# Edge attention in a four-layer graph kernel: masked maxima two steps further ahead, shifts in two operations, head sums normalised and added straight from PSUM

## The reference, cut to what matters

```python
s_u = x @ W_u.T + b_u
s_v = x @ W_v.T
e = s_u[src] + s_v[dst]
e = jnp.where(e >= 0, e, 0.2 * e)
m = jax.ops.segment_max(e, dst, num_segments=n_nodes)
e_exp = jnp.exp(e - m[dst])
denom = jax.ops.segment_sum(e_exp, dst, num_segments=n_nodes)
probs = e_exp / denom[dst]
xh = x.reshape(n_nodes, head_dim, num_heads)
msg = xh[src] * probs[:, None, :]
out = jax.ops.segment_sum(msg, dst, num_segments=n_nodes)
```

## Time and profile before

| What | Value |
|---|---|
| median of 3 runs | 995.82 us (993.37 to 998.53) |
| the profiled execution | 998.12 us, span 996.3 us |
| mean granted TensorE clock | 0.953 |
| PE / DVE / ACT / POOL busy over the span | 906.0 / 437.5 / 281.7 / 183.9 us |
| first copy of u (ACT) to the next layer's first operation on DVE | 525.4 to 608.9 us |

### The profile page before, as it was taken

The page is one execution under the profiler, slowest core; times in us unless marked ns, Lnnn a source line. Parts: engine busy times, 40 slices in busy tenths (PEclk is TensorE's granted clock), DMA queues, the critical chain, the costliest instruction groups (busy, mean ns, idle before and its releaser), DMA issues.

```text
span 996.3 us, 15288 instructions
## 1 busy us (share of the span) xinstructions
PE 906.0 (91%) x5607; PEld 730.9 (73%) x5607; DVE 437.5 (44%) x1375; ACT 281.7 (28%) x629; POOL 183.9 (18%) x179
## 2 busy tenths in 40 slices
PE   7999998999999999899997778999999998899895
PEld 7997656889999767788876667777886554565863
DVE  6687655522222421542278976423335242240422
ACT  5110362122222113233338952332112111114210
POOL 2100000122221100045317850000101100000231
PEclk9999999999999999999988988999999998799998
DMA  9202001288884603159341000354000000330694
GB/s 327 98 1 64 1 1 43 88 297 313 326 327 163 226 0 127 52 180 310 102 160 69 1 2 1 126 190 146 13 1 16 17 1 1 126 120 8 213 397 162
DMA packets 27452, 119.96 MB, mean 120 GB/s; under 512 B 5414, under 2 KB 9420, under 8 KB 19583
## 3 DMA queue, kind: packets, MB, share of 16 engines
q1 hardware_dynamic: 22012, 103.90, 29.3%
q0 software_dynamic: 5376, 15.20, 4.5%
HBM read 106.11 MB, written 12.98 MB: 120 GB/s over the span
## 4 chain that ended last, share of the span: by engine, by line
PE 75%; DVE 13%; DMA 4%; issue 4%; ACT 3%; POOL 1%; SPq 1%; DVEq 0%; POOLq 0%; ACTq 0%
PE PS L779 8%; PE PS L450 6%; PE PS L427 6%; PE PS L596 5%; PE PS L794 4%; PE PS L844 4%; PE PS L830 4%; PE PS L461 4%; PE PS L521 3%; PE PS L912 2%; PE PS L1213 2%; PE PS L866 2%; PE PS L901 2%; DVE ring L1904 2%; DVE w L1923 2%
## 5 line engine op out<-in xcount | busy, mean ns | idle before, releaser
L427 PE MATMUL PS<-const 128*128 128x128 f32 x726 | 98.9, 298 | 5.8 <-DVE X L1290 2.1
L427 PEld LDWEIGHTS PS<-const 128*128 128x128 f32 x726 | 94.4, 211 | 10.4 <-DVE X L1290 2.8
L779 PE MATMUL PS<-HT,ring 128*128 128x128 f32 x680 | 79.1, 275 | 3.3 <-DVE HT L1444 1.7
L779 PEld LDWEIGHTS PS<-HT,ring 128*128 128x128 f32 x680 | 78.4, 192 | 4.6 <-issue 3.9
L2548 POOL TENSOR_TENSOR col<-col,power 125x4 f32<-125x4 f32 (+2 forms) x13 | 11.9, 917 | 335.8 <-DVE col L1283 246.3
L2608 POOL DMA_INDIRECT slot_rows<-ST,route x43 | 43.4, 1009 | 154.7 <-ACT ST L2319 96.0
L2645 POOL TENSOR_TENSOR arena<-arena,ring 125x625 f32<-125x625 f32 x40 | 56.2, 1426 | 25.4 <-ACT arena L2406 13.0
L1829 DVE TENSOR_TENSOR HT<-HT,PS 128x256 f32<-128x256 f32 (+1 forms) x51 | 19.1, 377 | 89.8 <-ACT HT L2308 71.6
L596 PE MATMUL PS<-HT 125*125 125x250 bf16 x470 | 51.3, 270 | 1.0 <-DVE HT L1699 1.0
L596 PEld LDWEIGHTS PS<-HT 125*125 125x125 bf16 x470 | 50.2, 136 | 1.1 <-DVE HT L1699 1.1
L794 PE MATMUL PS<-ring,HT 128*128 128x256 f32 x204 | 46.8, 380 | 0.0
(11 more groups left out here) (460 smaller groups left out, 1691.4 us busy)
## 6 DMA issues: line engine op xcount, KB each, us to landing
ring<-in_experts SPq DMA_DIRECT2D x17, 1386.0 KB, 6.2
ring<-in_experts SPq DMA_DIRECT2D x17, 768.0 KB, 6.2
ring<-in_experts SPq DMA_DIRECT2D x11, 1026.0 KB, 7.7
arena<-in_experts SPq DMA_DIRECT2D x10, 1024.0 KB, 9.6
ring<-in_experts SPq DMA_DIRECT2D x7, 1024.0 KB, 8.2
arena<-in_experts SPq DMA_DIRECT2D x6, 1026.0 KB, 8.1
arena<-in_gnn SPq DMA_DIRECT2D x5, 1024.0 KB, 5.8
ring<-in_experts SPq DMA_DIRECT2D x8, 513.0 KB, 3.5
```

The costliest lines, as they stand in the source:

```text
L427: pe.matmul(PS[:, bank, 0:128], ident, ident, start=True, stop=True)
L779: mm = pe.matmul(PS[:, bank, at:at + SLOTS], both[:, j, k, m * 128:(m + 1) * 128], xs[0][i % 2][:, k, :], start=(k == 0), stop=(k == KD - 1))
```

## The change

Four things are changed, all in this stage.

1. The maxima of head h >= 3 start at DVE's step 5h-9, two steps earlier than before, and those of head 2 end one step earlier. Two waits are added for it, since buffers are reused sooner: a maximum waits for the POOL sum ten steps before it, and a head's shifts wait for the last exponential of the head two before it.
2. The shifts take two operations, and only the biased one is stored.
3. `take_y` and heads_y are gone. DVE reads the transposed sums in PSUM: for eight (head, tile) pairs one maximum and one reciprocal, then eight operations of 125 x 32 that multiply and add to X. This happens at DVE's steps 13, 21, 29 and 37, and for the last eight pairs behind the last count.
4. The last bank's transposes go to banks 1 and 0, where both went to bank 1.

```diff
@@ masked, shifts @@
                     dve.wait_ge(u_full, h + 2 if h else 1)
+                    if h >= 2:
+                        dve.wait_ge(bent_ready, i - 2 * NT + 1)
...
-                    link(dve.scalar_tensor_tensor(low[j][:, t0:t1], umax[j][:, t0:t1], -0.2, v08[:, t0:t1, h],
-                                                  ALU.mult, ALU.add))
-                    link(dve.scalar_tensor_tensor(shift[j][:, 0, t0:t1], umax[j][:, t0:t1], -1.0, low[j][:, t0:t1],
-                                                  ALU.mult, ALU.min))
-                    dve.tensor_tensor(shift[j][:, 1, t0:t1], shift[j][:, 0, t0:t1], v08[:, t0:t1, h],
-                                      ALU.subtract).then_inc(shift_ready, 1)
+                    if h >= 2:
+                        dve.wait_ge(gat_exp, NT * (h - 1))
+                    link(dve.scalar_tensor_tensor(low[j][:, t0:t1], umax[j][:, t0:t1], -1.0, v08[:, t0:t1, h],
+                                                  ALU.mult, ALU.subtract))
+                    dve.scalar_tensor_tensor(shift[j][:, t0:t1], umax[j][:, t0:t1], -0.2, low[j][:, t0:t1],
+                                             ALU.mult, ALU.min).then_inc(shift_ready, 1)
@@ normalise becomes add_sums @@
-                    link(dve.tensor_tensor(o, y[:, :, 0:32], rden.unsqueeze(2).broadcast_to([TP, b - a, 32]), ALU.mult))
-                    for h in range(h0, h1):
-                        xs = X[:, :, :].rearrange("p t (c h) -> p h t c", h=NX)[:, h]
-                        ins = dve.tensor_tensor(xs, xs, heads_y[:, h * NT:(h + 1) * NT, 0:32], ALU.add)
+                    xs = X[:, :, :].rearrange("p t (c h) -> p h t c", h=NX)
+                    for j in range(j0, j1):
+                        h, t = divmod(8 * b + j, NT)
+                        ins = dve.scalar_tensor_tensor(xs[:, h, t], y[:, j, 0:32], gate_flat[:, 120 + j:121 + j], xs[:, h, t],
+                                                       ALU.mult, ALU.add)
@@ DVE's order @@
-                ahead_of = {0: (5, 6), 1: (7, 8), 2: (9,)}
-                for h in range(2, NX):
+                ahead_of = {0: (5, 6), 1: (7, 8), 2: (9,), 3: (10, 11), 4: (12, 13), 5: (14,)}
+                for h in range(3, NX):
                     for j, ts in enumerate(((0, 1), (2,), (3,), (4,))):
-                        ahead_of[NT * h - 7 + j] = tuple(NT * h + t for t in ts)
+                        ahead_of[NT * h - 9 + j] = tuple(NT * h + t for t in ts)
...
-                    if i in (24, 32):
-                        dve.wait_ge(gat_y, i // 8 - 1)
-                        link(normalise_taken(i // 4 - 6, i // 4 - 4))
+                    if i >= 13 and i % 8 == 5:
+                        dve.wait_ge(gat_turned, i // 8)
+                        add_sums(i // 8 - 1, 0, 8).then_inc(gat_y, 1)
@@ ACT @@
-                    if i >= 12 and i % 8 == 4:
-                        take_y(i // 8 - 1, 8)
```

More of the change, by code:

```diff
@@ L274, in build @@
         XH = view(HT, 0, TP, NT, NX * 64)
-        heads_y = view(HT, NT * NX * 64, TP, NX * NT, 33)
         uvT = HT[0:40, 3900:3900 + N]
@@ L284, in build @@
         maskb = view(MB, 0, TP, NT, N)
-        shift = [view(col, 200 + 16 * j, TP, 2, NT) for j in range(2)]
+        shift = [col[:, 200 + 16 * j:200 + 16 * j + NT] for j in range(2)]
         gate_flat = gate[:, :, :, :].rearrange("p a t e -> p (a t e)")
@@ L1011, in turn_output @@
                     for k in pairs:
-                        mm = pe.transpose(PS[0:TP, b % 2 if b < 4 else 1, k * 128:(k + 1) * 128], sums_t[:, b % 2, k * TP:(k + 1) * TP],
+                        mm = pe.transpose(PS[0:TP, b % 2 if b < 4 else 1 - part, k * 128:(k + 1) * 128], sums_t[:, b % 2, k * TP:(k + 1) * TP],
                                           ident)
@@ L1924, in count_edges, with add_sums @@
                                       ALU.mult).then_inc(gat_pt, 1)
[L1926 to L1931, removed]
-                    link(dve.reciprocal(rden, den))
-                    link(dve.tensor_tensor(o, y[:, :, 0:32], rden.unsqueeze(2).broadcast_to([TP, b - a, 32]), ALU.mult))
-                    for h in range(h0, h1):
-                        xs = X[:, :, :].rearrange("p t (c h) -> p h t c", h=NX)[:, h]
-                        ins = dve.tensor_tensor(xs, xs, heads_y[:, h * NT:(h + 1) * NT, 0:32], ALU.add)
-                    return ins
-                def normalise_taken(h0, h1):
-                    return normalise(h0, h1, heads_y[:, h0 * NT:h1 * NT, :])
+                def add_sums(b, j0, j1):
+                    y = PS[0:TP, b % 2 if b < 4 else int(j0 == 0), :].rearrange("p (t c) -> p t c", c=64)
+                    den, rden = gate_flat[:, 80 + j0:80 + j1], gate_flat[:, 120 + j0:120 + j1]
+                    link(dve.tensor_scalar(den, y[:, j0:j1, 32], 1e-30, None, ALU.max))
+                    link(dve.reciprocal(rden, den))
+                    xs = X[:, :, :].rearrange("p t (c h) -> p h t c", h=NX)
[3 more added lines that the diff above has]
+                                                       ALU.mult, ALU.add)
+                    return ins
                 link(masked(0))
@@ L1965, in layer2_gnn @@
                             shifts(m // NT, 0, NT)
-                    if i in (24, 32):
-                        dve.wait_ge(gat_y, i // 8 - 1)
-                        link(normalise_taken(i // 4 - 6, i // 4 - 4))
+                    if i >= 13 and i % 8 == 5:
+                        dve.wait_ge(gat_turned, i // 8)
+                        add_sums(i // 8 - 1, 0, 8).then_inc(gat_y, 1)
                 count_edges(steps - 1)
[L1970 to L1973, removed]
+                dve.wait_ge(gat_turned, 5)
+                add_sums(4, 0, 6)
                 dve.wait_ge(gat_turned, 6)
-                ins = normalise(NX - 1, NX, PS[0:TP, 1, 192:512].rearrange("p (t c) -> p t c", t=NT))
+                ins = add_sums(4, 6, 8)
                 ins.then_inc(gat_taken, 1)
@@ L2413, in exponential @@
                         act.wait_ge(gat_tr, i - 2)
-                    act.activation(ex[:, i % 3, :], bent[:, i % 3, :], ACT.Exp, bias=shift[h % 2][:, 1, t:t + 1],
+                    act.activation(ex[:, i % 3, :], bent[:, i % 3, :], ACT.Exp, bias=shift[h % 2][:, t:t + 1],
                                    scale=0.2).then_inc(gat_exp, 1)
@@ L2423, in take_sums @@
                     act.activation(sums_t[:, b % 2, c0:c0 + c], PS[:, b % 2, c0:c0 + c], ACT.Copy).then_inc(gat_sums, 1)
[L2425 to L2430, removed]
                 for i in range(3):
@@ L2443, in layer2_gnn @@
                         take_sums(i // 8 - 1, 0, 4)
-                    if i >= 12 and i % 8 == 4:
-                        take_y(i // 8 - 1, 8)
                 take_sums(4, 0, 3)
-                take_y(4, 3)
                 take_sums(4, 3, 1)
```

## The result

| | before | changed |
|---|---|---|
| median of 8 runs | 994.99 us (992.78 to 999.12) | 1001.90 us (999.92 to 1006.58) |
| ratio | | 1.0063, 95% interval 1.0039 to 1.0088 |
| profiled execution, span | 998.12, 996.3 us | 999.92, 998.0 us |

The changed kernel is slower by 0.6%, 1001.9 us against 1001.8 predicted. That agreement is luck in part: the stage itself grew twice as much as forecast, and the rest of the program was shorter. In the table of the experiments, the medians and ratios leave out two executions that were in a slow state, one of e2 (4988.26 us) and one of e6 (1001.48 us).

A forecast was written before the change was run, and what follows sets the result against it. ACT and DVE were both full, PE set the pace at the end, and the new order made a ring bind. Terms -0.4 + 6.3 - 2.0 + 2.1 = +6.0 us on 995.82 gave 1001.8 us, range 990 to 1008.

The forecast's parts named there:

- The mechanism: At heads 3 to 7 DVE's earlier maxima wait for ACT's copy of u, 1 to 3 us each.
- the walk: Waits added through ACT, DVE and PE from one copy of u to the next: 10.4, 12.65, 9.56 and 12.6 us.
- The sum in the prediction: Copies of u for heads 3 to 7 span 45.2 us against 38.97 before, taken as +6.3.
- The term of 2.1 us: Two stretches of PE at 1.2 GHz, with one output each on the path, add 2.1 us.
- The tail: From the copy of u for head 7 to the next layer: 28.3 us against 30.28, so -2.0.
- The sums' price: On DVE, eight pairs with their maximum and reciprocal take 1.8 us; lower end 1.4, upper 3.45.
- the rival in which POOL slows them: DVE's small operations are slow beside POOL: eight pairs take 3.45 us instead of 1.8, total 1007.4 us; chance 0.13.
- my upper end: Upper bound for eight pairs on DVE: 3.45 us, what the first normalisation took beside POOL.
- The two rivals that would have made it faster or equal: Faster: the ring does not bind, 988.6 us, chance 0.14. Equal: gain and loss cancel, 996.1 us, chance 0.18.
- the ring: Loop from copy of u through DVE's counts, PE's turns and ACT's exponentials to the next copy: 9.5 us against 7.7.

The follow-up runs named there:

- e2: The changed kernel with the order of the maxima of before, parts 2 to 4 alone; stage 75.6 and 78.2 us, ratios to before 0.9883 and 0.9911.
- e6: The changed kernel with the sums' copy, transposes and additions to X two steps later on all three engines; stage 86.7 us, ratio to before 0.9968.
- e1: The kernel before with only the maxima two steps further ahead and the two waits that go with it; stage 100.3 us, ratio to before 1.0119.
- e3: The changed kernel with the copy of u for heads 3 to 7 two exponentials earlier on ACT; stage 85.1 us, ratio to before 0.9954.
- e5: The changed kernel with 16 idle products on PE at each of six waits, 96 in all; stage 91.7 us, ratio to before 1.0046.
- e8: e2 with each of the 40 small multiply-adds done twice, the extra result not used; stage 84.8 us, ratio to before 1.0035.

## Why the prediction was right, and where it was not

**The mechanism was right.** DVE waits for the copy of u at each of heads 4 to 7, 9.0 us in four waits (1 to 3 us each were forecast); at head 3 it waits 0.88 us, which the trace puts down to a POOL sum that ended as the copy did. Take_sums waited 2.52 us (2.3 walked). e1 and e2 show that the order is the loss, 17 us by itself and 17 to 20 us on top of e2, and e3 that the copy's place on ACT makes 10 us of it. For the other 7 to 9.5 us the walk has no wait of its own.

**The walk's waits.** For the heads 3 to 7 it had 10.4, 12.65, 9.56 and 12.6; the trace 10.8, 13.8, 11.0 and 14.8. The fillers, with the full clock, gave 9.56 and 12.50 for the last two, as walked. For the first two they don't bear it out: head 3 to 4 took 11.0 before the fillers began, at a clock of 0.85, and head 4 to 5 took 14.75, since the fillers themselves stood on its path. So two of the four lengths are confirmed. The sum in the prediction has a slip in it: 45.2 less 38.97 is 6.2, not 6.3.

**The clock was mis-sized.** The term of 2.1 us, two stretches with an output each, was too small by 2 to 6 us: the walk at the full clock gives 83.5 + 3.9 = 87.4 us for the stage, the trace 95.3, the difference is 7.9, and e5 gave 3.8 back net of its own products. The 4.1 us between the two are not assigned by any run. Not only outputs are slow in such a stretch: two turns took 2.46 us instead of 1.35, and I had counted none. There were also more stretches than two: over the whole stage the granted clock was 0.82 and 0.84 in the changed kernel, and 0.90, 0.90 and 0.88 in the kernel before.

**The tail** was 31.1 us against 28.3 walked, again with clock below full. The last addition did shorten the end: from the last count to the next layer are 3.8 us (612.23 to 616.05) against 4.8, 1.0 where I had 1.1.

**The sums' price was right**: 1.86 us against 1.8, and 0.18 us from one small operation to the next. At the first eight (550.45 to 552.31) POOL stood still from 550.60 to 552.15, so they don't settle the rival in which POOL slows them. The second eight do. Here they are, with POOL's row beside them:

```profile
572.34 0.16 DVE L1931 TENSOR_SCALAR gate<-PS 125x8 f32<-125x8 f32 x1
572.77 1.52 DVE L1936 SCALAR_TENSOR_TENSOR X<-PS,gate,X 125x32 f32<-125x32 f32 x8
572.37 2.71 POOL L2630 TENSOR_TENSOR arena<-arena,ring 125x625 f32<-125x625 f32 x2 [0.40 <-ACT arena L2401]
```

They took 1.52 us again, so that rival falls. The shifts, whose operands all lie in SBUF, were not spared: one of them took 1.21 us (at 580.55) and one 1.05 (at 591.57), both beside POOL, where most took 0.17. The prediction had them at 0.2 each. The Trainium skill's formula ("VectorE: DVE Perf Modes", section "The TRN2 errata") gave 1.5; the measurement decides, and lies between it and my upper end. What I did not see is that a block of that length costs more than itself where it stands ahead of late counts: e8 paid 2.5 us for 1.4, and e6 won 9 us by moving it together with the copy of sums.

**The sum agreed through the rest of the program.** I had +6.0 in the stage and nothing outside. It was +11.9 in the stage (95.3 against 83.5 in the means), and -6.2 outside in the profiles, which makes +5.6 in their spans and +6.9 in the medians. Two errors of 6 us cancelled, and that is luck. Of the first, the lower clock is at least 3.8 us, against the 2.1 that the forecast had for it. Of the second, about half arises in the first 20 us of the next layer, where the shorter last addition leaves PE standing 0.63 us instead of 1.61 and the clock stays higher. That gain goes with part 3 and lies outside the stage, where the prediction had nothing. The other half is open. It can be chance, since the rest of one kernel differed by 5.7 us between two profiles, and two and three profiles are few.

**The two rivals that would have made it faster or equal** fall with the first two points: at each of heads 4 to 7 DVE still stood for the copy.

## What to carry to other kernels

Taking work "further ahead" on one engine can help only if its input comes earlier too, and here even that was not enough (e3's stage was still 7 to 9.5 us longer than with the old order). Without it the waiting instruction holds back everything queued behind it, here the counts on which all other engines feed. Walk the ring once: from the producer through each engine's order back to the producer, and compare its length with the busiest engine's own work. When a change holds several edits, time the one that moves the order apart from the others: here three edits that together made the kernel 1% faster were hidden under one that made it slower. And look behind the stage that was changed: a gap of 1 us more or less at its end went with the clock of the next layer.

## What the runs showed of the hardware that I had not expected

The granted clock fell to its lower level behind PE's waits of 2 to 4 us for counts: after 4.24 us an output took 2.35 us instead of 1.29, and the window around it had a mean of 0.77. With 96 more products in the waits the clock was 1.00 from 550 us on. Identical code right behind the stage was granted 0.74 over 20 us in the five executions in which PE had stood 1.3 to 1.6 us ahead of it, and 0.83 or 0.91 in the nine in which it had stood 0.63. And a multiply-add of 32 columns from PSUM with X and a column of factors in SBUF kept its 0.27 us beside a running POOL, while the additions before, with both inputs in SBUF, took 2.79 us beside POOL for what is 0.80 in quiet (two at 588.80 and two at 605.77 in the trace of before).
